# Two shared units in place of three behind the expert tiles, rows of parts laid by group, VectorE's closing operations in another order

## The reference, cut to what matters

```python
x = x + tanh(g_xattn) * xattn(layernorm(x), ctx, mask, W, b)
h = layernorm(x)
top_logits, top_idx = top_k(h @ w_router, 2)          # 8 experts
scores = softmax(top_logits)
for e in range(8):                                      # a token's two experts
    proj, gate = split(h[rows of e] @ fc1_w[e], 2)
    out_e = silu(proj) * gate @ fc2_w[e]
moe = sum over a token's two rows of scores * out_e
shared = silu(h @ gate_w) * (h @ up_w) @ down_w        # inner size 512
x = x + tanh(g_ffn) * (moe + shared)
```

## Time and profile before

| | us |
|---|---|
| Median of 3 runs | 244.86 (244.76 to 245.46) |
| The profiled execution's own time | 244.42 |
| Its span, from the first to the last instruction | 242.7 |
| TensorE busy | 222.6 (92%) |
| VectorE busy | 174.8 (72%) |
| ScalarE busy | 130.7 (54%) |
| GpSimd busy | 123.1 (51%) |

### The profile page before, as it was taken

How to read it: one execution, slowest core, us unless ns; L and a number is a source line. 1 busy time by engine, 2 the same in 40 slices (tenths; PEclk the granted TensorE clock), 3 DMA queues, 4 the chain that set the end, 5 groups by cost and what they waited for, 6 DMA issues and landing times.

```text
span 242.7 us, 5276 instructions
## 1 busy us (share of the span) xinstructions
PE 222.6 (92%) x1421; PEld 195.1 (80%) x1421; DVE 174.8 (72%) x521; ACT 130.7 (54%) x316; POOL 123.1 (51%) x170
## 2 busy tenths in 40 slices
PE   7688999999699999889599999999999999998972
PEld 7677889988488888668488888888888888887861
DVE  1787799889458899899858566665665656655775
ACT  3365789773755545444125565665656656564420
POOL 1687787555788887888201343433434334344300
PEclk9999999999999999999899999999999999999999
DMA  6999930000131115522432434333343341147756
GB/s 174 277 393 405 405 119 0 0 3 22 45 112 66 66 66 178 173 71 88 105 97 78 122 92 127 89 103 113 88 131 89 87 123 45 48 136 253 221 225 248
DMA packets 18115, 32.05 MB, mean 132 GB/s; under 512 B 3030, under 2 KB 9307, under 8 KB 18088
## 3 DMA queue, kind: packets, MB, share of 16 engines
q1 hardware_dynamic: 14160, 22.42, 29.2%
q0 software_dynamic: 3408, 8.46, 9.3%
q10 hardware_dynamic: 520, 0.84, 1.0%
HBM read 19.95 MB, written 12.67 MB: 134 GB/s over the span
## 4 chain that ended last, share of the span: by engine, by line
PE 64%; DVE 19%; issue 6%; POOL 6%; ACT 2%; DMA 2%; another core or an unknown queue 0%; DVEq 0%; POOLq 0%
PE bank L975 47%; DVE ew_lo L244 6%; PE bank L1208 4%; PE bank L1228 4%; PE bank L1012 2%; DVE act L683 2%; DVE act_lo L622 2%; DMA acc<-in_x 2%; DVE acc L696 2%; PE bank L1039 1%; POOL rows L381 1%; POOL rs L322 1%; DVE acc L945 1%; PE bank L994 1%; POOL xn L334 1%
## 5 line engine op out<-in xcount | busy, mean ns | idle before, releaser
L425 POOL DMA_INDIRECT parts<-y_out,dst x39 | 38.8, 995 | 71.6 <-DVE dst L902 68.0
L908 DVE TENSOR_TENSOR act<-act,bank 128x256 f32<-128x256 f32 x39 | 16.4, 421 | 34.4 <-issue 24.3
L381 POOL DMA_INDIRECT rows<-hrows,slot x32 | 34.0, 1064 | 11.8 <-issue 11.5
L573 ACT ACTIVATE act<-bank 128x256 f32<-128x256 f32 x39 | 15.0, 384 | 37.0 <-PE bank L975 36.1
L975 PE MATMUL bank<-ew_hi,m_xt_hi 128*128 x78 | 31.1, 399 | 0.0
L975 PE MATMUL bank<-ew_hi,m_xt_lo 128*128 x78 | 30.8, 395 | 0.0
L975 PE MATMUL bank<-ew_lo,m_xt_hi 128*128 x78 | 30.8, 395 | 0.0
L975 PE MATMUL bank<-ew_hi,act_hi 128*128 x78 | 25.2, 323 | 0.2 <-DVE act_lo L622 0.2
L437 ACT ACTIVATE act_hi<-act 128x512 fp32r<-128x512 f32 x16 | 10.1, 631 | 23.6 <-DVE act L683 20.7
L975 PE MATMUL bank<-ew_hi,act_lo 128*128 x78 | 21.9, 281 | 0.0
L975 PE MATMUL bank<-ew_lo,act_hi 128*128 x78 | 21.9, 281 | 0.0
(11 more groups left out here) (180 smaller groups left out, 678.0 us busy)
## 6 DMA issues: line engine op xcount, KB each, us to landing
ew_raw<-in_chunks SPq DMA_DIRECT2D x12, 512.0 KB, 10.7
hrows<-rows SPq DMA_DIRECT2D x39, 130.0 KB
acc<-in_x SPq DMA_DIRECT2D x8, 256.0 KB, 4.2
low_buf<-parts SPq DMA_DIRECT2D x4, 512.0 KB, 6.0
high_buf<-parts SPq DMA_DIRECT2D x4, 512.0 KB, 7.6
sw_raw<-in_chunks SPq DMA_DIRECT2D x3, 512.0 KB, 8.2
out<-acc SPq DMA_DIRECT2D x3, 512.0 KB, 2.6
rows<-pad_rows SPq DMA_DIRECT2D x9, 130.0 KB
```

What stands on the lines that cost most here:

```text
L381: pool.indirect_dma_start(out=rows, out_offset=bass.IndirectOffsetOnAxis(ap=slot[:, h, k, i:i + 1], axis=0), in_=hrows[:, HT * h + i, :], ...
L425: pool.indirect_dma_start(out=parts, out_offset=bass.IndirectOffsetOnAxis(ap=dst[:, t:t + 1], axis=0), in_=y_out[:, t % SLOTS, :], in_offs ...
L573: a.activation(act[:, p, 0:I], M_H[p][:, 0:I], ACT.Silu).then_inc(s["m_sil"], 1)
L908: TT(act[:, p, 0:I], act[:, p, 0:I], M_H[p][:, I:2 * I], ALU.mult).then_inc(s["m_prod"], 1)
```

## The change

HELD goes from 3 to 2, so U0 from 13 to 14: unit 13 is done before the tiles and two units stay behind them. VectorE's and ScalarE's weight cuts are dealt out over one more unit (`LATER`, `more`). The tiles' PSUM banks change places with each other, since the pair of banks that the last unit before the tiles uses is the other one. VectorE's operations behind the tiles stand in another order. And the rows of `parts` are numbered by group, partition and place in the group (g, p, t), where they were by batch, partition and place (b, p, t); the token numbers that travel with the rows (`hrows[:, :, D]`) are counted the same way.

```diff
-HELD = 3
+HELD = 2
-LATER = {3: 1, 4: 1, 5: 1, 6: 1, 7: 1, 8: 2, 9: 2, 10: 3, 11: 3}
+LATER = {3: 1, 4: 1, 5: 1, 6: 1, 7: 1, 8: 1, 9: 2, 10: 2, 11: 2, 12: 3}
...
-    parts_v = parts.rearrange("(k b p t) d -> k b p t d", k=2, b=B, t=TB)
+    parts_v = parts.rearrange("(k g p t) d -> k g p t d", k=2, g=NS, t=ST)
...
-        M_H, M_Y, M_A, M_X = (bank[0], bank[1]), (bank[4], bank[7]), bank[3], bank[2]
+        M_H, M_Y, M_A, M_X = (bank[2], bank[3]), (bank[4], bank[7]), bank[1], bank[0]
...
-                    b, t = g // (NS // B), ST * (g % (NS // B))
-                    sp.dma_start(buf[:, ST * g:ST * g + ST, :], parts_v[part, b, :, t:t + ST, :])\
+                    sp.dma_start(buf[:, ST * g:ST * g + ST, :], parts_v[part, g])\
                         .then_inc(landed[g], 16)
...
-            pool.iota(hrows[:, :, D].rearrange("p (b t) -> p b t", b=B), pattern=[[S, B], [1, TB]], base=0,
-                      channel_multiplier=TB, allow_small_or_imprecise_dtypes=True).then_inc(s["const_r"], 1)
+            pool.iota(hrows[:, :, D].rearrange("p (g t) -> p g t", g=NS), pattern=[[SN, NS], [1, ST]], base=0,
+                      channel_multiplier=ST, allow_small_or_imprecise_dtypes=True).then_inc(s["const_r"], 1)
...
-                more = 3 if n < 8 else 2
+                more = 3 if n < 6 else 2
...
             add_low(0)
             add_low(1)
+            product(U0)
             add_low(2)
-            product(U0)
+            product_lo(U0)
+            add_high(0)
+            product(U0 + 1)
             add_low(3)
-            product_lo(U0)
-            product(U0 + 1)
             product_lo(U0 + 1)
-            add_high(0)
-            product(U0 + 2)
             add_high(1)
-            product_lo(U0 + 2)
             add_high(2)
             add_high(3)
...
             gate_up(U0 + 1)
             down(U0)
-            gate_up(U0 + 2)
             down(U0 + 1)
-            down(U0 + 2)
```

## The result

| | before | changed |
|---|---|---|
| Median of 13 runs each, us | 245.39 (244.28 to 249.64) | 244.14 (242.70 to 250.38) |
| The profiled execution's own time, us | 244.42 | 243.60 |
| Its span, us | 242.7 | 241.9 |

The ratio is 0.9932 [0.9906, 0.9959] (in brackets the 95% interval), so the change takes 1.7 us off (1.0 to 2.3). Two executions of each kernel ran several us longer at a lower granted clock (248.39 and 249.64, 250.31 and 250.38); they count in the medians, and the ratio leaves them out. The forecast was 243.8 us where the kernel before had a median of 244.86, a ratio of 0.9957. The direction is right, and the forecast's 1.1 us lies inside the interval.

A forecast was written before the change was run, and what follows sets the result against it. TensorE was taken to bound most of the kernel, except the way into the tiles and the end, which VectorE's chain sets. +1.05 - 2.1 = -1.1 us, so 244.86 - 1.1 = 243.8 us, range 242.5 to 245.4.

The forecast's parts named there:

- The end: Closing stage behind the tiles: VectorE's last add ends at 14.4 us instead of 16.5, a gain of 2.1 us.
- add_high(3) does not wait: Closing stage: the forecast had add_high(3) wait 0.2 to 0.5 us for its load, until t = 11.5.
- The order of the closing operations: VectorE's new sequence behind the tiles, worked out as a whole to end at t = 14.4, against 16.5 before.
- The rows' numbering: Layout of parts read by the high loads: taken at nothing; a 0.10 chance that it matters, half each way.
- The way in: Stretch before the expert tiles: the moved unit makes the tiles start 1.05 us late.
- a sign of being wrong: Way in: TensorE's tile start more than 0.5 us from 1.05 later than before would show the forecast wrong.
- I take nothing for it; it could give 0.7: Way in: one VectorE cut fewer behind unit 8 was counted as no gain, though up to 0.7 us was possible.
- The second is held to 117.2: Way in: VectorE's second cut behind unit 11 waits from 112.7 to 117.2 us for GpSimd's cuts.
- The half clock's price goes: Way in: the half clock's cost disappears, 1.0 us in down(11) and 0.5 in m_turn_x(1) and m_up(0).
- VectorE slips ahead of GpSimd: Way in, rival: VectorE's cuts escape or get between GpSimd's, giving 243.1 or 241.8 us; chance 0.17.
- The clock falls again: Way in, rival: idle before down(12) halves the clock, +1.5 us, giving 245.3 us; chance 0.15.
- First high load late: Closing stage, rival: first high load lands at t = 7.5, add_high(0) delays everything behind, 245.6 us; chance 0.08.

The follow-up runs named there:

- the better order: Changed kernel with add_low(2) put in front of product(14), add_low(3) behind it and add_high(1) ahead of product_lo(15): 242.67 us, 0.9869 to the kernel before.
- The pair with the stretch at half clock at the same place: Kernel before (three units) with new numbering and the better order, 243.68 us, against the better order with two units, 242.67 us.
- VectorE's six cuts: Changed kernel, GpSimd's last three weight cuts given to VectorE behind unit 12's product: 244.11 us, 0.9933; with the better order 243.03 us, 0.9861.
- the kernel before with the filling: Kernel before plus eight throwaway matmuls of 512 columns where TensorE waits for the first gathered rows: 245.83 us, 0.9972.
- The two fillings: Eight throwaway matmuls in TensorE's wait for gathered rows, added to two units with the better order (243.83 us, 0.9926) and to the kernel before (245.83 us, 0.9972).

## Why the prediction was right, point by point

**The end: the mechanism and the size hold.** The term was -2.1 us; the five profiles with two units, the changed or the old order and the new numbering have -2.5 (14.01 to 14.05 for 16.51). The pitches 0.60, 1.15 and 1.66 carried over to a few hundredths: the better order's 12.87 was worked out from them as 12.9 before it ran. What was 0.4 off is one sentence of the step: add_high(3) does not wait. I had its load at 8.5 us from one profile; in the twelve other kernels and the changed one the slowest landing is 6.0 to 7.7. With the load not late, the step's own working gives 14.1. Its split of the 2.1 is also off: it calls 1.4 the unit's VectorE work, and two operations of its own pitch of 0.60 are 1.2. The rest of the gain is waits. Before, VectorE waited 0.58 us in front of product(13) and then:

```profile
229.40 0.69 DVE L683 TENSOR_TENSOR act<-act,bank 128x512 f32<-128x512 f32 x1 [0.29 <-PE bank L975]
230.78 0.69 DVE L622 TENSOR_TENSOR act_lo<-act,act_hi 128x512 fp32r<-128x512 f32 x1 [0.70 <-ACT act_hi L437]
...
233.78 0.69 DVE L683 TENSOR_TENSOR act<-act,bank 128x512 f32<-128x512 f32 x1 [1.17 <-PE bank L975]
```

That is 2.74 us of waits, for the 1.72 of the changed kernel.

**The order of the closing operations.** I priced the whole order at once and so never asked what each part does. With two units, the old order gives 14.05 and the new 14.01. So the gain of the end is the unit's product and product_lo, and the waits that its absence closes; the order has no part in it that a profile shows.

**The rows' numbering.** Taken at nothing: 0.9975 [0.9937, 1.0013] alone. It holds for the time. It isn't nothing in the profile, see the last section. The rule on row pitches that the prediction weighed (the Trainium skill, DMA: Bandwidth & Descriptors, section Latency and other measured facts) has its figures for pitches of 512 KiB and more. At the 8 KB here the reads hardly differ: 3.9/5.4/6.8 us spread, 3.5/5.2/6.8 contiguous.

**The way in: the net came out near, its parts did not.** Forecast: +1.05, from +4.2 of matmul, -1.3 of idle and -1.5 of clock (these make 1.4; the other 0.35 is in starts that the rows of before have and the forecast's steps leave out, as the first turn's 0.41 us). Measured in the changed kernel's profile: +1.67, 0.62 off, which the prediction itself had named as a sign of being wrong. The pair with the stretch at half clock at the same place has +1.03, and that is luck: the forecast took 1.5 off for a half clock that goes, and in this pair both kernels pay it. Three steps failed.

- "I take nothing for it; it could give 0.7." In the changed kernel's profile the unit before the way in ended 2.3 us sooner (114.35 less the 1.4 of half clock in attention is 112.95, for 115.25). Windows of before and of the better order, both at full clock in this stretch (the first number behind the length is TensorE's busy time):

```profile
89.00:115.00 26.00, 23.88 (x135) 20.21 (x135) 24.05 (x49) 12.67 (x23) 21.26 (x20) 1.00 0.36 124
```

```profile
89.00:115.00 26.00, 25.76 (x146) 22.13 (x146) 24.48 (x51) 14.04 (x26) 21.39 (x18) 1.00 0.35 120
```

  1.88 us less idle. VectorE shows where it comes from. Before, then the better order:

```profile
96.66 1.95 DVE L880 TENSOR_TENSOR cmp<-e,t_exp 128x351 f32<-128x351 f32 x1
...
99.91 0.67 DVE L683 TENSOR_TENSOR act<-act,bank 128x512 f32<-128x512 f32 x1
...
103.62 0.69 DVE L683 TENSOR_TENSOR act<-act,bank 128x512 f32<-128x512 f32 x1 [0.99 <-remote]
...
108.01 0.68 DVE L683 TENSOR_TENSOR act<-act,bank 128x512 f32<-128x512 f32 x1
```

```profile
99.28 0.68 DVE L682 TENSOR_TENSOR act<-act,bank 128x512 f32<-128x512 f32 x1
...
101.31 0.68 DVE L682 TENSOR_TENSOR act<-act,bank 128x512 f32<-128x512 f32 x1
...
105.53 0.68 DVE L682 TENSOR_TENSOR act<-act,bank 128x512 f32<-128x512 f32 x1
```

  The last product here stands 2.48 us sooner. 0.63 is already there at 99.28, since the operation of 96.66, which took 1.95 us beside a GpSimd cut of 96.88, met none there. Of the 1.68 up to the next product 0.72 is a cut less behind unit 8, and 0.99 a wait that is gone. That the meetings with GpSimd's single cuts shift was not worked out, though the earlier trace rows show what one costs.

  But this is how these two profiles went, and not what the moved unit does. Counted from unit 6's product, this work ends at 26.14 before and at 23.8 in these two. In the six other profiles with two units and the same cuts up to here it ends at 25.65 to 26.00, and TensorE waits 1.0 to 1.4 us for an act_lo, as it waited 0.99 at 108.15 before. And the kernel before with the filling, which has three units, gets there at 24.35. So "I take nothing" held in six profiles of eight. What it left out is that the meetings of VectorE with GpSimd's single cuts shift from one profile to the next, with three units as with two.

- "The second is held to 117.2." In the changed kernel's profile GpSimd's last scatters came later, its cuts at 116.53 for 112.88, and the hold fell on unit 12's third cut. The idle came out at 2.35 + 0.24 us, for the 1.65 forecast. With the 1.4 of half clock in attention taken off, act_lo ended at 120.2, sooner than the forecast's 121.3, and the rows landed at 119.6, where the prediction had "landed at 117.4": TensorE came early and then waited for the rows. This eats 0.9 of the 2.3 gained. Late rows are no mark of two units either: counted from unit 6's product, GpSimd's last cuts start at 23.8 us in the kernel before, at 23.9 to 26.0 in the eight profiles with two units that have them, and at 25.7 in two of the four with three. Why GpSimd's scatters take more time in one profile than in another was not looked into.

- "The half clock's price goes." At this place it went in the changed kernel, but the stretch at 35.1 cost 1.4. From the first turn to the third, without the idle inside, before takes 123.45 - 117.41 - 0.97 = 5.07 us; the kernel with the old numbering, at full clock, 3.77. So the price of the clock there is 1.3. Counted again from unit 6's product, so that earlier half clock is left out, T stands at 134.55 - 1.3 = 133.25 us before and at 134.82 in the changed kernel. It stands at 135.10 to 135.48 in five others that are at full clock from there (the old numbering, the old order, the better order with the old numbering, and VectorE's six cuts with either order). That is +1.6 to +2.2; the better order's profile, with its own half clock of 1.1 taken off, has +1.3. The forecast without its clock term was 1.05 + 1.5 = +2.55. So the moved unit costs less at equal clock than I thought, and how much of it the clock gives back differs from profile to profile.

**The sum.** In the profile +1.67 - 2.50 = -0.83 for a forecast of -1.05: the two terms missed by 0.6 and 0.4 with opposite signs, so a part of the net's nearness is luck. The runs say -1.7 (-2.3 to -1.0), a little more than either. A straight line through the runs that the ratios compare (0.49 us of time per us lost to the clock, which is the span times one less the granted clock; the slope is the same for all kernels) puts the changed kernel 1.4 +- 0.4 us under before at equal clock. So the gain isn't luck with the clock. That the profiles at equal clock give less, between 0.3 and 0.9 (+1.6 to +2.2 and -2.5), stays open: there is one profile of each kernel, and the way in differs from one to the next.

**The rivals.** "VectorE slips ahead of GpSimd": no. The changed kernel's third cut was due at 116.4, 0.1 us ahead of GpSimd's start at 116.53, and was held. In twelve of the fourteen profiles there are VectorE cuts, product_lo and comparisons with both inputs in SBUF that start 0.04 to 0.60 us ahead of a GpSimd cut by the records, and each of them was held until GpSimd was through. So the rule of the Trainium skill (SBUF: State Buffer, section Who interferes with whom), by which whoever issues first has the pair, disagrees with every such case here, unless starts are recorded late on GpSimd. "The clock falls again": not in this profile, but in the better order's it did, with the same idle (2.37 us before 119.55) in front. I gave 0.15; it fell there in 1 of 10 profiles with two units, so most of the time this part of the forecast stands. "First high load late": no; it would need to land later than t = 5.4, and only the old numbering with two units comes that late (5.8, and 0.46 lost).

## What to carry to other kernels

Work out a closing stage by the pitches of the engine that ends it, and try each independent operation in each wait: here one add moved into a 1.72 us wait was worth 1.1 us, where putting all of them in another order was worth 0.04. Price a moved unit at both ends at equal clock, and read at least two profiles before a landing or a half-clock stretch of one becomes a term. Two engines that hold each other up want a timeline of both: when one thing ahead of them shifts, the holds fall on other instructions, and they shift from one profile to the next without any change.

## What the runs showed of the hardware

- **VectorE and GpSimd on cuts with both inputs in SBUF.** Six cuts on VectorE alone took 4.31 us; three, while GpSimd did three, took 5.85 to 5.98. Giving GpSimd half of this work made VectorE slower than doing all of it. A VectorE operation of this kind that starts up to 0.6 us ahead of GpSimd's cuts is held for the whole run of them: 4.40 to 4.53 us for one of 0.69 in front of three cuts, 1.9 to 2.5 in front of one.
- **The clock.** Stretches at 0.50 fell at 35, 46, 66 or 119 us in otherwise equal kernels, the one at 35 behind 2 us in which TensorE was busy for 1.74 (first window of the changed kernel). In all four profiles with three units behind the tiles one began between 119.0 and 121.6; in one of ten with two units. What starts them was not settled. The two fillings don't tell: one kernel had perhaps no idle to fill, and in the other 3.86 us of idle stood behind the filling.
- **The numbering and the scatters.** SyncE's first high load started between 0.61 us ahead of T and 0.04 ahead in the ten profiles with rows numbered by group, and 0.48 to 1.78 behind T in the four with the old numbering. In the three pairs that differ in the numbering alone the loads start 1.3, 1.4 and 2.1 us sooner with the new one. In the program SyncE waits there for the scatters to `parts`, so it is these that seem to land sooner. In only one kernel did the old numbering's later loads cost time, 0.46 us at its end. The mechanism was not looked into.
